# First attention: the band put on the exponentials by GpSimd, no NF4 plane folded, eight of fifteen NF4 comparisons as signs on ScalarE

## The reference, cut to what matters

```python
# attention over 512 positions, 8 heads of 16, 16 examples
scores = jnp.einsum('bqhd,bkhd->bhqk', q, k) / jnp.sqrt(jnp.asarray(d, q.dtype))
idx = jnp.arange(t)
band = jnp.abs(idx[:, None] - idx[None, :]) <= local_size      # local_size = 64
neg = jnp.asarray(jnp.finfo(scores.dtype).min, scores.dtype)
scores = jnp.where(band[None, None], scores, neg)
attn = jax.nn.softmax(scores, axis=-1)
o = jnp.einsum('bhqk,bkhd->bqhd', attn, v).reshape(n, t, e)
...
# NF4: each weight, divided by its block's maximum, goes to the nearest of 16 levels
scaled = (blocks / scalers_1[:, None]).reshape(-1)
idx = jnp.argmin(jnp.abs(scaled[:, None] - NF4), axis=-1).astype(jnp.uint8)
...
first = NF4[(packed >> 4).astype(jnp.int32)]
```

## Time and profile before

| | |
|---|---|
| Runs | 1453.96 us median of 3 (1452.56 to 1455.08) |
| The profiled execution | 1457.34 us, of which the span is 1455.5 us |
| The phase that is changed | from the start to about 478 us of the span |
| PE busy over the span | 93%; DVE 67%, ACT 54%, POOL 17% |
| Granted TensorE clock, mean | 0.975 |

### The profile page before, as it was taken

One profiled execution on the slowest core, in us unless ns is written; L12 is line 12 of the kernel. 1 busy time (PEld: TensorE's weight loads), 2 busy tenths in 40 slices (PEclk: granted clock), 3 DMA queues, 4 the chain that ended last, 5 costly groups with the idle time before them and its releaser, 6 DMA issues. The chain is left out here.

```text
span 1455.5 us, 28759 instructions
## 1 busy us (share of the span) xinstructions
PE 1360.6 (93%) x8732; PEld 823.0 (57%) x8732; DVE 981.9 (67%) x3234; ACT 788.3 (54%) x1802; POOL 249.0 (17%) x265
## 2 busy tenths in 40 slices
PE   3688999999999899999989999998788999999998
PEld 1345655556555544444455555555334778777774
DVE  8888999999986545546456788877569555444111
ACT  4777888888878533232367666767420233333231
POOL 4100000000000100000020001004211355555442
PEclk7699999999999999999999999999999999999999
DMA  8543343434430400000020000000513588989885
GB/s 265 142 99 91 90 117 95 122 96 105 114 82 10 145 0 0 0 0 1 1 75 15 16 16 14 14 1 30 184 42 113 172 250 255 253 250 254 228 238 115
DMA packets 63187, 149.52 MB, mean 103 GB/s; under 512 B 10793, under 2 KB 27831, under 8 KB 58893
## 3 DMA queue, kind: packets, MB, share of 16 engines
q1 hardware_dynamic: 49836, 115.70, 26.4%
q0 software_dynamic: 13280, 32.93, 9.7%
HBM read 113.21 MB, written 35.39 MB: 102 GB/s over the span
## 5 line engine op out<-in xcount | busy, mean ns | idle before, releaser
L775 DVE CUSTOM_DVE_ANT_0 masked_scores<-ps_max,band_mask 128x192 bf16<-128x192 f32 (+1 forms) x512 | 177.0, 382 | 17.6 <-PE ps_max L506 12.5
L384 ACT ACTIVATE probs_t<-ps_sc 128x448 f32<-128x448 f32 x256 | 139.1, 544 | 70.3 <-PE ps_sc L526 70.1
L378 ACT ACTIVATE nf_above<-nf_scaled,nf_sign_at 128x512 f16<-128x512 bf16 x231 | 161.9, 717 | 0.0
L1254 PE MATMUL f_ps<-f_xt,w_t 128*128 (+1 forms) x704 | 158.5, 379 | 1.5 <-ACT w_t L1309 1.5
L2802 DVE TENSOR_TENSOR d_inter<-d_silu_g,d_su 128x384 f32<-128x384 f32 x32 | 17.7, 554 | 167.1 <-PE d_su L2486 159.6
L1926 ACT ACTIVATE c_probs<-d_sg,c_negmax 128x128 f32<-128x128 f32 x256 | 90.3, 364 | 58.0 <-DVE c_negmax L2011 57.6
L1254 PEld LDWEIGHTS f_ps<-f_xt,w_t 128*128 128x128 bf16 x704 | 68.9, 98 | 84.4 <-issue 1.7
L2319 POOL DMA_INDIRECT out<-d_h,d_scatter_now x64 | 97.4, 1522 | 109.5 <-DMA out<-d_h,d_scatter_now 92.6
L506 PE MATMUL ps_max<-k_stack,q_stack 96*128 96x192 bf16 (+1 forms) x512 | 96.2, 271 | 19.7 <-DVE row_max L775 13.4
L2670 DVE TENSOR_SCALAR d_onehot<-d_slot_no,d_pos 128x192 bf16<-128x192 bf16 x512 | 99.2, 285 | 0.3 <-PE d_lb L2387 0.3
L2480 PE MATMUL d_su<-d_h,d_wgu 128*128 128x192 f32 x512 | 94.2, 339 | 1.4 <-DVE d_h L2789 1.1
(11 more groups left out here) (385 smaller groups left out, 2891.9 us busy)
## 6 DMA issues: line engine op xcount, KB each, us to landing
d_wgu<-in_ex_gu SPq DMA_DIRECT2D x32, 1024.0 KB
d_wdown<-in_ex_d SPq DMA_DIRECT2D x32, 512.0 KB
dr_parts<-qk_parts SPq DMA_DIRECT2D x32, 384.0 KB, 4.6
q_stack<-dr_parts SPq DMA_DIRECT2D x32, 192.0 KB, 2.7
k_stack<-dr_parts SPq DMA_DIRECT2D x32, 192.0 KB, 3.3
out<-x_sb SPq DMA_DIRECT2D x21, 256.0 KB, 2.1
nf_w<-in_nf_w POOLq DMA_DIRECT2D x3, 1408.0 KB, 9.8
q_stack<-dr_parts SPq DMA_DIRECT2D x32, 128.0 KB, 2.4
```

The costliest lines, as they stand in the source:

```text
L378: act.activation(above[:, g, k, :], lvl[:, g, :], ACT.Sign, bias=cut[:, k - NDV:k - NDV + 1]).then_inc(s_sg, 1)
L384: act.activation(pt[:, c, :], SP[c % 2][:].rearrange("p a w -> p (a w)")[:, a:z], ACT.Exp, scale=D0 ** -0.5).then_inc(s_e, 1)
L775: op = dve.tensor_tensor_reduce(masked[:, c % 2, k, off:off + hi - lo], M[c % 2][:, k, off:off + hi - lo], mask[:, k, off:off + hi - lo], ...
L1254: mm = pe.matmul(bank[:], w12[:, m, kt, ft * P:(ft + 1) * P], xt[:, q, kt, bass.ds(g * N, N)], start=(kt == 0 and q == 0), stop=(kt == KT ...
```

## The change

GpSimd gets a new job, `band(u, c)`: for each step it waits for the exponential and sets everything outside the band to 0 in place, by two `affine_select` of 128 x 256 f32 elements (the lower edge of both tiles, then the upper). The mask matmul L521 goes. `pv` waits for the new semaphore `a_probs_in_band` in place of `a_exp`. `probs_t` becomes [128, 8, 2, 256], and GpSimd zeroes its unused margins once. On the NF4 side threshold 7 moves from DVE to ACT (`NDV` 8 to 7), the addition of planes 1 and 3 goes, and PE adds up all 15 planes. GpSimd's four small transfers now stand between its bands.

```diff
-NDV = 8
+NDV = 7
-    pt = sb("probs_t", [P, 8, 2 * WIN - BAND], F32)
+    pt = sb("probs_t", [P, 8, 2, WIN], F32)
-    NF_INC = 5
+    NF_INC = 4
-    SIGN_AT = [[[8], [9, 10], [], [], [], [11], [12], [13, 14]], [[8], [9], [10], [], [11], [12], [13], [14]]]
+    SIGN_AT = [[[7], [8, 9], [10], [], [], [11], [12], [13, 14]], [[7, 8], [9], [10], [], [11], [12], [13], [14]]]
 # GpSimd
+            def band(u, c):
+                pool.wait_ge(s_e, 8 * u + c + 1)
+                pool.nop(nofuse=True)
+                low, high = pt[:, c, :, 0:P], pt[:, c, :, P:WIN]
+                pool.affine_select(out=low, in_=low, compare_op=ALU.is_ge, fill=0.0, base=0,
+                                   pattern=[[0, 2], [1, P]], channel_multiplier=-1)
+                pool.affine_select(out=high, in_=high, compare_op=ALU.is_ge, fill=0.0, base=0,
+                                   pattern=[[0, 2], [-1, P]], channel_multiplier=1).then_inc(s_in, 1)
+            def body(j, i, b, first, last, final):
+                for c in range(8):
+                    band(2 * i, c)
+                if first:
+                    pool.wait_ge(s_sc, 1)
+                    spread_scales(0, 1)
+                for c in range(8):
+                    band(2 * i + 1, c)
+                    if c == 4 and isinstance(i, int) and i == 1:
+                        pool.wait_ge(s_sc, 2)
+                        spread_scales(1, 3)
+                if first:
+                    pool.wait_ge(s_am, 5)
+                    gather_maxima(1, 3)
...
 # TensorE
-                a, z = kept(kp)
-                pe.matmul(s[:].rearrange("p a w -> p (a w)")[:, a:z], identb[:],
-                          mask[:].rearrange("p a w -> p (a w)")[:, a:z], start=True, stop=False)
-                                   qst[0:98, b, h, lo:hi], start=False, stop=(k == 1))
+                                   qst[0:98, b, h, lo:hi], start=True, stop=True)
-                pe.wait_ge(s_e, 8 * u + 4 * kp + 4)
+                pe.wait_ge(s_in, 8 * u + 4 * kp + 4)
-            NF_KS = [0, 2] + list(range(4, NLV))
-            NF_AT = [[], [], [0, 2], [4, 5], [6, 7], [8, 9], [10, 11], [12, 13, 14]]
+            NF_KS = list(range(NLV))
+            NF_AT = [[], [], [0, 1], [2, 3, 4], [5, 6, 7], [8, 9, 10], [11, 12], [13, 14]]
 # VectorE
-                    for k in range(2 * c, 2 * c + 2):
+                    for k in range(2 * c, min(2 * c + 2, NDV)):
-                if c == 4:
-                    dve.wait_ge(s_ab, NF_INC * m + 4)
-                    dve.tensor_tensor(above[:, g, 0:4:2, :], above[:, g, 0:4:2, :], above[:, g, 1:4:2, :], ALU.add).then_inc(s_ab, 1)
```

More of the change, by code:

```diff
@@ L174, in phase_layer0_attention @@
     s_s, s_e, s_pv = sem("a_scores"), sem("a_exp"), sem("a_pv")
+    s_in, s_pad = sem("a_probs_in_band"), sem("a_probs_pad")
     s_oc, s_oT, s_rs, s_on = sem("a_o_copy"), sem("a_o_turn"), sem("a_o_recip"), sem("a_o_norm")
@@ L337, in _ @@
             load_nf(2)
[L338 to L343, removed]
+            def band(u, c):
[20 more added lines that the diff above has]
+                    gather_maxima(1, 3)
+            pool.wait_ge(s_ko, 1)
+            pool.memset(pt[:, 0:4, 0, 0:BAND], 0.0).then_inc(s_pad, 1)
+            pool.wait_ge(s_pad, 1)
+            pool.memset(pt[:, 4:8, 1, WIN - BAND:WIN], 0.0).then_inc(s_pad, 1)
+            pool.wait_ge(s_pad, 2)
+            batches(pool, body)
         @block.scalar
@@ L383, in exps @@
                 a, z = kept(c // 4)
-                act.activation(pt[:, c, :], SP[c % 2][:].rearrange("p a w -> p (a w)")[:, a:z], ACT.Exp, scale=D0 ** -0.5).then_inc(s_e, 1)
+                act.activation(pt[:, c].rearrange("p a w -> p (a w)")[:, a:z], SP[c % 2][:].rearrange("p a w -> p (a w)")[:, a:z], ACT.Exp, scale=D0 ** -0.5).then_inc(s_e, 1)
             def o_copy(u, g):
@@ L538, in pv @@
                         mm = pe.matmul(O[32 * j:32 * j + 32, lo:hi], va[:, b, kt, 4 * g + j, :],
-                                       pt[:, 4 * kp + j, k * WIN + off - kept(kp)[0]:k * WIN + off - kept(kp)[0] + hi - lo],
+                                       pt[:, 4 * kp + j, k, off:off + hi - lo],
                                        start=(kt == 0), stop=(kt == QT - 1), skip_group_check=True)
```

## The result

| | before | after |
|---|---|---|
| Runs, median | 1453.99 us (1451.36 to 1457.15, 16 runs) | 1459.93 us (1455.88 to 1463.83, 16 runs) |
| Ratio after to before | | 1.0043, 95% interval 1.0035 to 1.0051 |
| The profiled execution | 1457.34 us | 1461.07 us, span 1458.5 us |
| Granted TensorE clock, mean | 0.975 | 0.979 |

The change makes the kernel 0.43% slower, where 1.2% faster was forecast. The forecast, rivals 1 to 3 and the range 1425 to 1453 all missed, and rival 4, the slower one, put it at 1467.

A forecast was written before the change was run, and what follows sets the result against it. PE bounds the kernel before, DVE and ACT close behind; DVE was to bound after. Eleven and a half examples at -1.4 (-16.1) and smaller terms give -18.1: 1453.96 to 1436 us, range 1425 to 1453.

The forecast's parts named there:

- rivals 1 to 3: PE bounds, 1428 us, chance 0.20; DVE pays more, 1449, 0.14; bands late for every pv, 1449, 0.07.
- rival 4: Comparison trains at steps 0 to 3 wait for full bands, DVE bounds: 1467 us; chance 0.17 shared with slow selects.
- I add 0.15: 23.8 us per example: Eleven examples: DVE longest at 23.65, plus 0.15 for late steps between engines, against 25.20 before.
- PE's sum: PE per example: 25.14, less 3.12 for mask matmuls, plus 0.87 for added planes, gives 22.9 us.
- DVE's sum without selects: DVE per example: 23.76 less 1.60 for two comparisons and two plane additions, 22.15 us.
- What the selects cost: DVE's comparison trains (L907) delayed by POOL's selects: some 1.5 us per example, between bounds 0 and 6.2.
- Two inputs in SBUF: DVE operations with two SBUF inputs beside selects: priced at nothing; if delayed, five at 0.2 each, +1.0 per example.
- rival 2: DVE's five two-input operations delayed, or trains pay 0.35 each: DVE 24.65 to 24.8 per example, 1449 us; chance 0.14.
- The added wait: pv of an even unit's steps 4 to 7 waits for its band: some 0.2 us once per example, counted as nothing.
- rival 3: Bands 0.5 late at all four pv, PE's waits naming probs_t from POOL: 24.9 per example, 1449 us; chance 0.07.
- POOL's queue: Example 1: bands of steps 5 to 7 stand behind the spreading of scales; pv waits 1 us, once.
- The last example: No row maxima, so ACT bounds: 19.3, with small waits 19.5, against 20.40 us: -0.9.

The follow-up runs named there:

- e8: The kernel before, unchanged, run and profiled once more: 1452.96 us, ratio 1.0002 to before.
- e3: The kernel after without any select, pv waiting for the exponential: 1447.02 us, ratio 0.9953 to before.
- e2: The kernel before with the NF4 edits alone; mask matmul stays on PE, no selects on GpSimd: 1465.21 us, ratio 1.0081 to before.
- e13: The kernel after without selects, with the three planes of PE's step 5 moved ahead to steps 2 to 4: 1440.27 us, ratio 0.9911 to before.
- e7: The kernel after without selects, with DVE's comparisons spread one per step over steps 0 to 6: 1442.74 us, ratio 0.9918 to before.
- e14: The kernel after without selects, comparisons spread over steps 0 to 6 and PE's step 5 planes moved ahead: 1442.75 us, ratio 0.9926 to before.
- e1: The kernel after with the NF4 edits undone, so the band on GpSimd alone: 1456.08 us, ratio 1.0015 to before.
- e5: The kernel after with its seven DVE comparisons spread, one at each of steps 0 to 6: 1452.25 us, ratio 0.9988 to before.
- e6: The kernel after with the three planes of PE's step 5 moved ahead to steps 2, 3 and 4: 1446.68 us, ratio 0.9949 to before.
- e10: The kernel after with comparisons spread over steps 0 to 6 and PE's step 5 planes moved ahead: 1450.46 us, ratio 0.9979 to before.
- e4: The kernel after with selects on a scratch tile and pv waiting for the exponential: 1462.82 us, ratio 1.0071 to before.

## Why the prediction was wrong, point by point

The terms against the two profiled executions, in us:

| stretch | forecast | measured |
|---|---|---|
| up to the eleven examples | -1.5 | -1.9 |
| the eleven examples | -15.4 | +2.4 |
| example 14 | -1.2 | -0.65 |
| the last example | -0.9 | +1.7 |
| the end of the phase | +0.9 | +1.0 |
| the rest of the program | 0 | +1.1 (scatter, by e8) |
| sum | -18.1 | +3.7 |

**The step that failed** is "I add 0.15: 23.8 us per example", by which the pace was the longest sum of an engine and little more. It carries 1.39 of the 1.62 us per example that were missed: without selects the kernel should have run at 22.9 + 0.15 = 23.05 and ran at 24.44 (e3). That PE's own work is 22.9 is borne out by e2, where PE is full: 25.91 less the 16 mask matmuls at 0.19 is 22.87. Each engine's sum had room, but not in the same steps. From the earlier trace rows I took DVE's 1.44 us of idle time as room anywhere. Four windows of one example of the kernel before say otherwise:

```profile
core 0: us, PE busy (x) PEld busy (x) DVE busy (x) ACT busy (x) POOL busy (x), PEclk, DMA share, GB/s
270.70:278.20 7.50, 7.50 (x58) 4.54 (x56) 7.36 (x34) 6.22 (x12) 0.00 (x0) 1.00 0.22 54
278.20:283.20 5.00, 5.00 (x48) 3.15 (x46) 4.97 (x19) 4.12 (x8) 0.00 (x0) 1.00 0.16 54
283.20:290.80 7.60, 7.54 (x67) 4.26 (x69) 7.57 (x35) 7.06 (x15) 0.00 (x0) 1.00 0.79 194
290.80:295.80 5.00, 5.00 (x42) 3.08 (x33) 3.83 (x17) 3.91 (x8) 0.00 (x0) 1.00 0.36 97
```

For 20.1 us in a row DVE is busy for 19.90, as full as PE; nearly all its room lies in the last 5 us. What PE gives up in the first three windows can be used only as far as DVE gives up work there too, and in the fourth, which begins with the end of the step with pv (to which the change adds a plane), PE is the bound alone. Of the 1.39 us the place of the three planes is shown to hold 0.73 (e13 against e3), and the place of the comparisons 0.42 (e7 against e3); with both moved the pace is 24.00 (e14), so the two don't add. What holds the last 0.66 of e13, 23.71 against 23.05, is open.

**PE's sum.** 22.9 could not be read off, since a matmul's duration counts in full before a wait (0.35 against a pitch of 0.19) and there are more waits now; busy is 23.5. The four planes cost 0.71 per example where PE is full (e2), for 0.87 forecast.

**ACT.** Forecast 22.6, measured 22.5. Right, and never the bound.

**DVE's sum without selects.** Forecast 22.15, measured 22.11 (e3). Right in size, with some luck: the same instructions come to 22.35 in e7, with the comparisons spread, and e2, also without selects, has 22.60.

**What the selects cost.** Their direct effect on DVE was put at 1.5; the busy time went from 22.11 to 23.19, so 1.08. Pairs of comparisons of 0.83 and 0.92 us agree with the exclusion of the earlier trace rows. To the pace they were to add 23.8 - 23.05 = 0.75 and added 0.98, the other 0.23 of the miss. The effect depends on which instructions meet: 0.53 in e1 (against the kernel before) and 0.52 in e5 (against e7), 0.85 in e6 (against e13), 1.2 in e10 (against e14). So does the effect on the pace: 0.98 here, 0.21, 0.49 and 0.35 in those last three pairs.

**Two inputs in SBUF.** I priced these at nothing by the earlier trace rows and said that the trace disagrees with the Trainium skill (SBUF — State Buffer, "Who interferes with whom"). DVE's own operations are indeed hardly longer in the kernel after (L921 has a mean of 677 ns, 684 before; L774 one of 691, 675 before). But GpSimd's are. In all engines' timeline of the kernel after:

```profile
357.04 0.69 DVE L774 TENSOR_TENSOR qk_parts<-qk_resid,qk_parts 128x512 bf16<-128x512 f32 x1
...
357.07 0.92 POOL L345 TENSOR_SCALAR_AFFINE_SELECT probs_t<-probs_t 128x256 f32<-128x256 f32 x1 [1.30 <-ACT probs_t L411]
...
358.20 0.70 DVE L774 TENSOR_TENSOR qk_parts<-qk_resid,qk_parts 128x512 bf16<-128x512 f32 x1
358.31 0.85 POOL L345 TENSOR_SCALAR_AFFINE_SELECT probs_t<-probs_t 128x256 f32<-128x256 f32 x1
...
359.12 0.40 POOL L347 TENSOR_SCALAR_AFFINE_SELECT probs_t<-probs_t 128x256 f32<-128x256 f32 x1
...
359.57 0.96 PE L562 MATMUL ps_o<-probs_t,v_ones 128*32 128x256 f32 x16 [0.65 <-POOL probs_t L347]
```

Two selects take 0.92 and 0.85 us in place of 0.41, and the band is late for pv. The rule holds here, and GpSimd pays, which started 0.03 and 0.11 us behind DVE. The earlier trace rows had shown this already, and I read only DVE's half of it: one addition L2056 falls into that stretch, and the operation of POOL that started 0.22 us behind it is the one with the longest time of its line, 2.40 in place of 2.07. From the timelines of DVE and POOL of the kernel before:

```profile
1008.13 0.68 DVE L2056 TENSOR_TENSOR x_sb<-x_sb,c_out 128x512 f32<-128x512 f32 x1
...
1008.35 2.40 POOL L1607 TENSOR_SCALAR c_next_rows<-x_sb,c_next_mv,c_next_rstd 128x512 f32<-128x512 f32 x1
```

Where DVE starts second, DVE pays. In all engines' timeline of e10:

```profile
307.82 0.53 POOL L345 TENSOR_SCALAR_AFFINE_SELECT probs_t<-probs_t 128x256 f32<-128x256 f32 x1 [0.77 <-ACT probs_t L411]
308.01 0.88 DVE L921 SCALAR_TENSOR_TENSOR nf_scaled<-nf_w,absmax_recip 128x512 bf16 x1
...
308.31 0.85 POOL L347 TENSOR_SCALAR_AFFINE_SELECT probs_t<-probs_t 128x256 f32<-128x256 f32 x1
```

There L921 has a median of 887 ns, against 677 in the kernel after; a select is running at the start of each of the 22 scalings in e10's eleven examples, and of none in the kernel after's. These are the 0.2 each of rival 2, for two of its five operations. Twice 0.21 is 0.42 us per example, about the 0.36 by which e10's DVE is busier than e6's. For the kernel after the 24.65 that the rule gave for DVE was no better than my 23.65: 23.19 was measured.

**The added wait.** Forecast 0.2 us once per example, counted as nothing; measured 0.65, and by e4 worth 0.03. The size was wrong, the conclusion right. The sign that was set for rival 3, PE's waits naming probs_t from POOL, did come, but at one pv of an example's four, and by e4 it is not what costs: rival 3 is out. The two selects beside L774 run 0.95 us over their 0.82 together, more than the 0.45 by which the wait was missed.

**POOL.** Forecast 0.39 for a select and 14.4 us per example; measured medians 0.407 and 0.406, and 14.6. Right.

**POOL's queue.** Forecast 1 us for pv in example 1; measured 2.16 (before pv at 116.30), behind the scales' transfers, whose issue ends at 114.05 (115.31 in the kernel before). Right in kind, and twice as long.

**The last example.** I let ACT bound it with 19.3 and small waits. ACT is busy for 19.4, but of 22.12 us: PE waits for exponentials and bands, ACT for scores. Without selects it took 21.19 (e3), and without selects but with planes early 20.23 (e13): without selects the place of the planes is worth 1.0 us, and the bands cost 0.9. With selects the place of the planes gives only 0.2 there (21.92 in e6).

**Rival 4**, the slower one, came nearest in time, with the wrong mechanism: DVE was not full, and the selects' direct cost was 1.08 and not the 3.05 from which it was to decide.

The best version is e6, 1446.68 us: 0.51% under the kernel before (0.32 to 0.69%), and about 0.9% under the kernel after.

## What to carry to other kernels

When an engine that is full in every step gives up work, ask for each stretch of the loop, not for the loop as a whole, how full the others are: in this kernel, with two tiles between PE and DVE, room did not carry over from one stretch to the next. After such a change look for places where A waits for B and, a few steps on, B waits for A; then move work that is free to move out of the step that is waited for, and count the time of a wait as lost only after an experiment takes it away (0.65 us per example of pv's wait were worth 0.03).

## What the runs showed of the hardware that was not expected

- A GpSimd select of 128 x 256 f32 that starts 0.03 to 0.16 us after a DVE operation with two SBUF inputs takes 0.78 to 0.92 us in place of 0.41, and the DVE operation keeps its 0.68 to 0.70. Where the select starts first, by 0.19 us, the DVE operation takes 0.88 (e10).
- A pair of DVE comparisons (one SBUF input, 0.49 us alone) takes 0.83 and 0.92 us beside two selects.
- With the same instructions in another order the selects' cost to DVE's busy time ranges from 0.52 to 1.20 us per example.
- PE stopped for 1.2 to 2.5 us in the middle of one pv of example 14 in most of the profiled executions, with nothing shown that it waited for. After the stops of 1.84 us in e4 and 2.49 us in e5 the granted clock was 0.58 for some 4 us and 0.50 for some 6 us.
